# The scan pass of a state-space layer: delta*u through every eighth partition, and C in one transfer placed by ScalarE

## The reference

```python
delta = jnp.einsum('kblr,krc->kblc', dpart, dt_w) + dt_b[:, None, None, :]
delta = jax.nn.softplus(delta + dt_b[:, None, None, :])
A_neg = -jnp.exp(A_logs)
def step(state, inp):
    d, b, c, uu = inp
    dA = jnp.exp(d[..., None] * A_neg[:, None, :, :])
    state = dA * state + (d * uu)[..., None] * b[:, :, None, :]
    y = jnp.einsum('kbcn,kbn->kbc', state, c)
    return (state, y)
```

## Time and profile before

| | us |
|---|---|
| Median of 3 executions | 18105.77 (18101.2 to 18110.01) |
| The profiled execution | 18079.56 |
| Its span, first to last instruction | 18077.9 |
| The scan pass's units in it (line 1713), first to last | 8540.6 to 16441.7 |
| PE busy, whole span | 14837.0 |
| DVE busy | 11267.9 |
| ACT busy | 7510.9 |
| POOL busy | 6783.4 |

### The profile page before, as it was taken

The page is one execution under the profiler, slowest core; times in us unless marked ns, Lnnn a source line. Parts: engine busy times, 40 slices in busy tenths (PEclk is TensorE's granted clock), DMA queues, the critical chain, the costliest instruction groups (busy, mean ns, idle before and its releaser), DMA issues. The chain is left out here.

```text
span 18077.9 us, 359613 instructions
## 1 busy us (share of the span) xinstructions
PE 14837.0 (82%) x130080; PEld 10962.3 (61%) x130080; DVE 11267.9 (62%) x10440; ACT 7510.9 (42%) x12873; POOL 6783.4 (38%) x3199
## 2 busy tenths in 40 slices
PE   7899997999989745444888888888888888888899
PEld 5666665666666412222767767776777667765467
DVE  5666666666666555554777766766777667765532
ACT  4444444444444354444444444444444444442200
POOL 1000000000000042334777767766777667773100
PEclk9999998999999877776777777777777777777799
DMA  5222222222222276668889999999999999998711
GB/s 118 67 60 59 56 56 68 56 56 62 56 67 51 87 182 151 160 163 203 209 209 211 209 209 208 208 206 208 210 210 210 209 209 210 210 209 213 218 37 43
DMA packets 1692803, 2640.24 MB, mean 146 GB/s; under 512 B 1081676, under 2 KB 1245260, under 8 KB 1667404
## 3 DMA queue, kind: packets, MB, share of 16 engines
q1 hardware_dynamic: 1645388, 2493.45, 58.5%
q0 software_dynamic: 12288, 86.71, 2.2%
q10 hardware_dynamic: 34944, 57.81, 1.1%
HBM read 2110.03 MB, written 556.32 MB: 147 GB/s over the span
## 5 line engine op out<-in xcount | busy, mean ns | idle before, releaser
L1713 DVE TENSOR_TENSOR_SCAN L2.h<-L2.ps,L2.db 128x912 f32<-128x912 f32 x2688 | 5514.7, 2056 | 2415.4 <-POOL L2.db L1578 2311.1
L1578 POOL TENSOR_TENSOR L2.db<-L2.du,L2.bt 128x896 f32<-128x896 f32 x2688 | 5582.1, 2095 | 2395.1 <-DMA L2.du<-du 2298.4
L1601 PE MATMUL L2.ps<-L2.dm,L2.wa 32*128 32x112 f32 (+2 forms) x24192 | 4480.3, 343 | 1176.2 <-DVE L2.h L1713 1045.2
L1601 PEld LDWEIGHTS L2.ps<-L2.dm,L2.wa 32*128 32x128 f32 x24192 | 4123.2, 255 | 1889.1 <-DVE L2.h L1713 1352.2
L1653 ACT ACTIVATE L2.ps<-L2.ps 128x896 f32<-128x896 f32 x2688 | 2425.9, 902 | 4603.0 <-PE L2.ps L1601 4601.7
L1613 PE MATMUL L2.ps<-L2.h,L2.cd 128*8 128x96 f32 x50176 | 2575.9, 362 | 4.2 <-DVE L2.h L1713 4.2
L1613 PEld LDWEIGHTS L2.ps<-L2.h,L2.cd 128*8 128x8 f32 x50176 | 1441.3, 108 | 584.4 <-DVE L2.h L1713 4.3
L314 POOL TENSOR_TENSOR L1.x_res<-L1.x_res,L1.ob 96x3136 f32 (+1 forms) x16 | 95.4, 5976 | 2582.4 <-ACT L1.qv L457 2582.4
L366 PE MATMUL L0.p_proj<-L0.xt,L0.w_hi 128*96 128x448 f32 x3024 | 825.8, 383 | 195.1 <-DVE L0.xt L560 168.5
L366 PE MATMUL L1.p_proj<-L1.xt,L1.w_hi 128*96 128x448 f32 x3024 | 826.1, 383 | 194.4 <-DVE L1.xt L560 167.8
L314 POOL TENSOR_TENSOR L0.x_res<-L0.x_res,L0.ob 96x3136 f32 (+1 forms) x16 | 95.8, 6006 | 2369.5 <-ACT L0.qv L457 2369.5
(11 more groups left out here) (255 smaller groups left out, 19228.5 us busy)
## 6 DMA issues: line engine op xcount, KB each, us to landing
L2.du<-du SPq DMA_DIRECT2D x2688, 448.0 KB, 11.1
L2.dm<-d SPq DMA_DIRECT2D x896, 336.0 KB, 11.0
y<-L2.ysum SPq DMA_DIRECT2D x896, 84.0 KB
L0.left<-table SPq DMA_DIRECT2D x48, 1176.0 KB
L0.right<-table SPq DMA_DIRECT2D x48, 1176.0 KB
L1.left<-table SPq DMA_DIRECT2D x48, 1176.0 KB
L1.right<-table SPq DMA_DIRECT2D x48, 1176.0 KB
du<-L2p.work SPq DMA_DIRECT2D x64, 784.0 KB, 7.6
```

The lines of the kernel that those rows point to most:

```text
L1578: pool.tensor_tensor(db[:, n % RB, :, 2:ROW], du[:, n % RD, :].rearrange("p (c t) -> p c t", t=SPAN), row, ALU.mult)\
L1601: mm = pe.matmul(decays[n % RA][:, a:b], wa[rows, j, :], dm[rows, j, a - lo:b - lo], start=True, stop=True)
L1713: dve.tensor_tensor_scan(h[:, half, u * UNIT:(u + 1) * UNIT, :].rearrange("p c t -> p (c t)"), decays[n % RA], db[:, n % RB, :, :].rearran ...
```

## The change

Delta*u takes two steps. `load_few` brings a unit's 16 rows (8 images, 2 copies) once each from memory into `few`, one row in every eighth partition, 3 slots. `spread_du` then copies from there, SBUF to SBUF, each row to 8 partitions of the du slot, of which there are now 4. SyncE issues a spread only when its `few` has landed; and before it issues the load of unit n + 2 (`next_few`), it waits until the spread of unit n - 1 has landed, since that frees the `few` slot. C comes once per block instead of once per half, in one transfer of 128 partitions (`load_cc`). ScalarE then makes cd from it with eight instructions of 128 x 112 that scale by a column of `image`, ones in the partitions of image b and zeros elsewhere (`make_cd`), at the end of the block's first half. VectorE's clearing of cd goes, and TensorE waits for the made cd instead of the loaded one.

```diff
-def scan_layer(nc, sems, tag, wa_dram, d_dram, du_dram, bc_dram, y_dram):
+def scan_layer(nc, sems, tag, ap, wa_dram, d_dram, du_dram, bc_dram, y_dram):
...
     with m.ctx:
-        RA, RB, RD = 3, 3, 6
+        RA, RB, RC, RD = 3, 3, 3, 4
         FILLS = 7
...
         bt = m.sb("bt", [128, 2, SPAN])
-        cd = m.sb("cd", [128, 2, BATCH, SPAN])
+        cc = m.sb("cc", [128, SPAN])
+        cd = m.sb("cd", [128, BATCH, SPAN])
+        image = m.sb("image", [128, BATCH])
+        few = m.sb("few", [128, RC, UNIT * SPAN])
         du = m.sb("du", [128, RD, UNIT * SPAN])
...
         bt_in = [m.sem(f"bt_in{s}") for s in range(2)]
-        cd_in = [m.sem(f"cd_in{s}") for s in range(2)]
+        image_in = m.sem("image_in")
+        cc_in = m.sem("cc_in")
+        cd_made = m.sem("cd_made")
+        few_in = [m.sem(f"few_in{s}") for s in range(RC)]
         du_in = [m.sem(f"du_in{s}") for s in range(RD)]
...
-            def load_cd(k, s, half):
-                for b in range(BATCH):
-                    sp.dma_start(cd[STATES * b:STATES * (b + 1), half, b, :], bc_dram[1, k, b, :, span_of(s)]).then_inc(cd_in[half], 16)
-            def load_du(k, s, half, u):
-                c = half * HALF + u * UNIT
+            def load_cc(k, s):
+                sp.dma_start(cc[:], bc_dram[1, k].rearrange("b n t -> (b n) t")[:, span_of(s)]).then_inc(cc_in, 16)
+            def load_few(k, s, n):
+                c = n * UNIT
                 rows = du_dram[k, :, :, 0:NSPANS * CH * SPAN].rearrange("b o (s n) -> (b o) s n", s=NSPANS)
...
                     rows[:, bass.ds(s, 1), c * SPAN:(c + UNIT) * SPAN].rearrange("r a n -> r (a n)")
+                sp.dma_start(few[0:128:BATCH, n % RC, :], rows).then_inc(few_in[n % RC], 16)
+            def spread_du(k, s, n):
+                sp.wait_ge(few_in[n % RC], count(sp, k, s, 32 * UNITS // RC, 16 * (n // RC + 1)))
+                rows = few[0:128:BATCH, n % RC, :]
                 src = bass.AP(tensor=rows.tensor, offset=rows.offset,
-                              ap=[list(rows.ap[0]), [0, STATES // COPIES], list(rows.ap[1])])
-                sp.dma_start(du[:, (half * UNITS + u) % RD, :], src).then_inc(du_in[(half * UNITS + u) % RD], 16)
+                              ap=[list(rows.ap[0]), [0, BATCH], list(rows.ap[1])])
+                sp.dma_start(du[:, n % RD, :], src).then_inc(du_in[n % RD], 16)
+            def next_few(k, s, n, later):
+                landed = count(sp, k, s, 32 * UNITS // RD, 16 * ((n - 1) // RD + 1))
+                if not (isinstance(landed, int) and landed == 0):
+                    sp.wait_ge(du_in[(n - 1) % RD], landed)
+                steady(sp)
+                if n + 2 < 2 * UNITS:
+                    load_few(k, s, n + 2)
+                elif later is not None:
+                    load_few(*later, n + 2 - 2 * UNITS)
...
                     steady(sp)
-                    load_du(k, s, half, u)
+                    spread_du(k, s, half * UNITS + u)
+                    next_few(k, s, half * UNITS + u, later)
                     if u == 2 and earlier is not None:
...
                         store_y(*earlier, half)
-                    if u == 3:
-                        if not (isinstance(fills, int) and fills == 0):
-                            sp.wait_ge(sum_ready, fills)
+                    if u == 3 and half == 0:
+                        made = count(sp, k, s, BATCH)
+                        if not (isinstance(made, int) and made == 0):
+                            sp.wait_ge(cd_made, made)
                         steady(sp)
-                        load_cd(k, s, half)
+                        load_cc(k, s)
                     if u == 4 and table is not None:
...
             sp.wait_ge(cleared, 1)
+            sp.dma_start(image[:], ap["c_image"]).then_inc(image_in, 16)
             load_wa(0, 0)
...
             load_wa(0, 1)
+            for n in range(2):
+                load_few(0, 0, n)
             for k in range(DIRS):
...
                         t = SPAN // 4 * q + FROWS * f + i
-                        mm = pe.matmul(ps[32 * q:32 * q + BATCH, bank, i * HALF:(i + 1) * HALF], cd[:, half, :, t],
+                        mm = pe.matmul(ps[32 * q:32 * q + BATCH, bank, i * HALF:(i + 1) * HALF], cd[:, :, t],
                                        h[:, half, :, 2 + t], start=True, stop=True)
...
                             pe.wait_ge(scanned, units + (half * UNITS + RB))
-                            pe.wait_ge(cd_in[1 - half], count(pe, k, s, 128, 128 * half))
+                            if half:
+                                pe.wait_ge(cd_made, count(pe, k, s, BATCH, BATCH))
                         sum_states(1 - half, f, before)
...
             pe.wait_ge(scanned, DIRS * HALVES * UNITS + RB)
-            pe.wait_ge(cd_in[1], 128 * DIRS * NSPANS)
             for f in range(FILLS):
...
             act.wait_ge(cleared, 1)
+            act.wait_ge(image_in, 16)
+            def make_cd(k, s, fills):
+                act.wait_ge(cc_in, count(act, k, s, 16, 16))
+                act.wait_ge(sum_ready, fills + 2 * FILLS)
+                for b in range(BATCH):
+                    act.activation(cd[:, b, :], cc[:], ACT.Identity, scale=image[:, b:b + 1]).then_inc(cd_made, 1)
...
                         take_sum(k - 1 if begun and half == 0 else k, 1 - half, f, before)
+                if half == 0:
+                    make_cd(k, s, before)
...
             dve.memset(db[:], 0.0)
-            dve.memset(cd[:], 0.0)
             dve.memset(zero[:], 0.0)
...
     out["c_parts"] = np.stack([p % 2 == 0, p % 2 == 1], 1).astype(np.float32)
+    out["c_image"] = (p[:, None] // STATES == np.arange(BATCH)).astype(np.float32)
     out["c_diag"] = (p[:, None] // 2 % BATCH == np.arange(BATCH)).astype(np.float32)
...
         prep_layer(nc, None, "L2p", x2, ap, z, xc, d, du, bc, consts)
-        scan_layer(nc, None, "L2", wa, d, du, bc, y)
+        scan_layer(nc, None, "L2", ap, wa, d, du, bc, y)
         fin_layer(nc, None, "L2f", x2, x3, ap, z, xc, y, consts)
```

## The result

| | before | after |
|---|---|---|
| Median us | 18103.49 (18094.73 to 18110.01, 4 runs) | 20779.27 (20776.25 to 20780.77, 4 runs) |
| Ratio | 1 | 1.1478 [1.1458, 1.1498] |
| Span of the profiled execution | 18077.9 | 20778.7 |
| First to last scan of the pass | 7901 | 10587 |
| us a block (that / 112) | 70.55 | 94.53 |

What follows compares the result with a forecast made beforehand. It took the DMA engines as the bound: 63.9 - 42.5 + 52.9 + 6.6 - 0.3 = 80.6 us busy plus 1.4 idle, 82.0 a block against 70.55, plus 1282 us, about 19390 us; range 18050 to 20200.

Steps and rivals of the forecast that it cites:

- the sign: Whole kernel: the change makes it slower, plus 1282 us in the forecast; chance of slower 0.81.
- which wait grows: Scan pass: GpSimd's wait for delta*u, handed on to VectorE, still leads, with more than 2298 us.
- the spread's rate: SBUF to SBUF copy of delta*u: 208 GB/s, the middle row, 2.21 us each, plus 52.9 us a block.
- The two rivals with a free spread: Delta*u copy at 259 GB/s: 18550 us, chance 0.18; at 407 GB/s: about 17600 us, chance 0.15.
- the rival of 16 neighbours: Delta*u copy: sixteen sources behave like sixteen neighbours, 112 GB/s, 132 us a block, about 25000 us; chance 0.03.
- the term for idle time: DMA engines in the scan pass: 1.4 us a block kept as idle, added to the busy sum.
- SyncE's queue: Issue loop with two spreads in flight: 72 us a block, 85 with dm; the DMA sum lies inside this.
- the busy time: DMA engines in the scan pass: 80.6 us busy a block, from 63.9 before.
- RD from 6 to 4 costs nothing: Delta*u slots: fewer cost nothing beyond the wait, as two in flight never fill four buffers.
- y's slow stores: Rival: y's stores at 50 GB/s, up to 9.4 us a block more; half counted, 19950 us; chance 0.17.
- C and ScalarE: C's gap in SyncE's queue goes, transfers minus 0.3 us a block; placements about 0.25 us each, delaying scan up to 2.
- The profile test: Window of spreads: 208 GB/s with DMA share under 90% means the landing wait limits and the idle term is too small.

Runs made afterwards that it cites:

- stride1: Changed kernel with the 16 rows of the small load in partitions 0 to 15 instead of every eighth: 25209.92 us, ratio 1.3929.
- stride4: Changed kernel with the 16 rows of the small load in every fourth of partitions 0 to 63: 20720.75 us, ratio 1.1441.
- y_cut: Changed kernel with each y store cut to 1 of 28 tokens, same number of issues: 19630.79 us, ratio 1.085.
- c_two: c_rd4 plus the wait: after each delta*u load SyncE waits until the load before it has landed; no copy: 20076.69 us, ratio 1.11.
- c_rd4: c_only with 4 instead of 6 slots for delta*u, loaded from memory: 18043.54 us, ratio 0.9975.
- mix4: mix with 4 slots for the small loads, each issued four units ahead of its spread instead of two: 18032.6 us, ratio 0.9961.
- c_only: The C part of the change alone on the kernel before, delta*u loaded from memory into six slots: 17662.66 us, ratio 0.9761.
- deep_wide: deep with each row kept twice, in every fourth of all 128 partitions, each copied to 4 instead of 8: 18586.95 us, ratio 1.0265.
- deep_stride7: deep with the 16 rows in every seventh partition, 0 to 105: 19849.32 us, ratio 1.096.
- mix: C part with odd units copied from 32 partitions and even ones loaded from memory, six du slots, small loads two units ahead: 18962.11 us, ratio 1.0489.
- deep: Changed kernel with six slots for the small loads, SyncE waiting for the spread four back instead of one: 19833.96 us, ratio 1.096.

## Why the prediction was wrong

**Right: the sign, and which wait grows.** A transfer ends last, GpSimd and VectorE hand on its wait, and the wait in that place more than doubled, from 2298 to 5095 us. What bounds it is another thing: the forecast rested on the DMA engines' busy time, at a share of 95% or more, and the share is 77.9%.

**Right in number: the spread's rate.** 208 GB/s was taken from the middle row; the windows show 213, and stride1 shows that a crowded side sets the speed. The reason given, how much of the partition array is touched, is not the one: stride4 touches half as much of it and is as fast. The port rule of the Trainium skill (SBUF — State Buffer, section Door 1: The DMA port swizzle), which the prediction cites with 218 GB/s, puts both on 8 ports. The two rivals with a free spread (259 and 407 GB/s) were wrong in their premise. So was the rival of 16 neighbours for this change. It put a block at 132 us, all of it busy, and stride1, which is that case, took 134.1; that is luck, as the engines are busy 86.5% of it, 116 us, and 18 are idle.

**Wrong: the term for idle time, and with it SyncE's queue.** This is the step that failed. The prediction worked out a loop of 72 us of units plus 13.2 of dm, 85 a block, then wrote that the DMA sum "lies inside this" and kept 82.0 with 1.4 idle; 20.9 us a block were idle. Two things are wrong in it. A loop of 85 us is a floor, and a sum of 80.6 below it doesn't pull it down: taking the larger of the two would have given 85. That alone is 19724 us, still 1055 short of the measured 20779. And y's stores, also issued in that loop, were left out of it: only what they would cost more at 50 GB/s, 9.4 us a block, stands in a rival, and there by half. At the whole price of the earlier trace rows they are 2 x 6.9 = 13.8, and the loop 72 + 13.2 + 13.8 = 99.0 us; 94.53 was measured. The timeline has for the same parts: twelve pairs of units at 5.0, 60 and not 72 (a pair takes 5.0, not 6.0); dm 8 x 2.1 = 17; y 2 x 8.5 = 17 (y_cut takes 10.1 of it away and leaves the eight issues). So the units were priced too high, dm and y too low. But the form, a serial loop whose parts add, is what the queue shows, and c_two shows the wait's size with no copy present: 18.1 us a block.

**Wrong, and it hid in the other direction: the busy time**, 73.6 and not 80.6. Idle time was 19.5 us a block too small and busy time 7.0 too large, which leaves the 12.5 by which the forecast of 82.0 missed. The packets' times, added up by size in the two traces and shared out over 16 engines and 112 blocks, say where. Packets of 3584 bytes, the du loads before and the spreads with their small loads after, take 45.3 us a block before and 55.0 after; the prediction had 42.5 and 59.5. So the term removed was 2.8 too small and the two added were 4.5 too large. dm's packets (13.2 before, 11.5 after) and y's (3.1 and 5.2) nearly cancel.

**Half right: "RD from 6 to 4 costs nothing".** Beside the wait it seems so, as SyncE in after and in c_two waits nowhere for a free slot, though no run has the wait with six slots. Taken by itself it costs 3.4 us a block, which c_rd4 shows. The 18.1 were measured on top of that.

**Half right: y's slow stores.** The mechanism was named as a rival, with its cause put at the crowded read side. The store does go at 41 GB/s. But the cause was named wrongly. One us of c_two, where no spread exists, and one of mix4, where half of the units are spreads, say so (stores alone, c_two first):

```profile
DMA packets 117, 0.04 MB, mean 43 GB/s; under 512 B 117, under 2 KB 117, under 8 KB 117
```

```profile
DMA packets 375, 0.14 MB, mean 139 GB/s; under 512 B 375, under 2 KB 375, under 8 KB 375
```

Slow stores go with the shallow queue, not with the spread. The row for it was the earlier trace rows, the same stores with nothing queued before them: it foretold this, and only its use was too timid.

**Right: C and ScalarE.** C's gap goes: 3.8 us a block, against 4.7 for its gap and 0.3 for its transfers. A placement takes 0.376 us and not 0.25, inside the bounds given, and is mostly covered: VectorE waits for ScalarE's copy of the state 118 us in all, where it did 54 before. In c_only, where the other cover is smaller, it is 189 us, 1.2 us a block more than before and inside the 2 us named; the C part as a whole gains.

**The profile test was right.** The prediction said that 208 GB/s in a window of spreads, with a DMA share under 90%, would mean that the wait for landing is the limit and the idle term too small. It was 213 GB/s and 77.9%.

## What to carry to other kernels

When an edit adds a wait for a landed transfer to the queue that issues everything, write out that queue as a serial loop, with every transfer issued in it at its price with little queued before it; the loop is a floor, not a correction to the engines' sum. Copying within SBUF took no load off the DMA engines here: the bytes delivered stay and a fan-out adds the first step's bytes. Reading from more partitions and a deeper queue each took back part of the loss, but no version with a copy beat c_only, which loads from memory. Try the parts of a change apart: here one half alone gained 2.4%, and the other alone cost 18.3%.

## What the runs showed of the hardware

- **Repeated reads of the same rows in SBUF slow down when the rows are crowded.** The times of all packets of 3584 bytes (small loads among them) pile up at a few values: 140 ns is the most frequent in deep_wide (median 159), the spreads of after stand around 285 (median of all 262), those of stride1 around 552 (median of all 552). By the Trainium skill's port rule, cited above, 16 engines reading at 16, 8 and 4 ports are 1, 2 and 4 to a port, an estimate that fits these three. deep_stride7, at 14 ports with a median of 251, does not fit it. From issue to landing a spread takes 4.7 us in deep_wide (median), 5.6 in after and 8.7 in stride1.
- **Small stores were fast only with much queued before them.** Over the whole pass y's packets of 384 bytes take a mean of 27.7 ns in the kernel before, 28.8 in c_only, 28.5 in mix4, 35.4 in c_rd4, 43.4 in mix, 46.6 in after, 46.5 in c_two and 47.2 in deep. In mix4 SyncE waits for landings too (1609 us), so it is not the waiting as such. In windows of one to three us the stores pass at 138 GB/s before and 41 to 44 in after, c_two and deep. One us each of c_only and c_rd4:

```profile
DMA packets 326, 0.12 MB, mean 120 GB/s; under 512 B 326, under 2 KB 326, under 8 KB 326
```

```profile
DMA packets 154, 0.06 MB, mean 58 GB/s; under 512 B 154, under 2 KB 154, under 8 KB 154
```

  By the Trainium skill, SBUF — State Buffer, section Door 1: The DMA port swizzle, the 32 partitions that y's four stores read (0 to 7 and the same 32, 64 and 96 further) are 4 ports, and the estimate is about 109 GB/s; 138 is above that. Why the stores slow down, and why they can pass that estimate, no run here tests; it stays open.
- **dm's packets are shorter with a shallow queue.** It writes 64 neighbouring partitions. Its packets of 5376 bytes take 398 ns in the kernel before (median), but 253 to 265 in the kernels in which SyncE waits for a landed delta*u transfer (256 in after, 255 in c_two). The mean falls less, from 414 to 362 in after and 328 in c_two, as some packets get longer. It was not tried alone and stays open.
